# Causal mask for layer 2's row maxima: from TensorE mask products into VectorE's maximum instruction

## What is computed

```python
att = jnp.einsum('bhqd,bhkd->bhqk', q, k) / jnp.sqrt(jnp.float32(D))
mask = jnp.tril(jnp.ones((t, t), dtype=bool))
att = jnp.where(mask, att, jnp.float32(-jnp.inf))
att = jax.nn.softmax(att, axis=-1)
y = jnp.einsum('bhqk,bhkd->bhqd', att, v)
```

## Time and profile before

| | |
|---|---|
| runs of the kernel before | 652.36, 646.97, 653.94 us; median 652.36 |
| the profiled execution, device time | 647.78 us |
| its span, first to last instruction | 646.1 us |
| PE busy | 549.5 us (85%) |
| DVE busy | 396.2 us (61%) |
| ACT busy | 309.1 us (48%) |
| POOL busy | 212.8 us (33%) |
| mean granted TensorE clock | 0.943 |

### The profile page before, as it was taken

The page is one execution under the profiler, slowest core; times in us unless marked ns, Lnnn a source line. Parts: engine busy times, 40 slices in busy tenths (PEclk is TensorE's granted clock), DMA queues, the critical chain, the costliest instruction groups (busy, mean ns, idle before and its releaser), DMA issues.

```text
span 646.1 us, 10027 instructions
## 1 busy us (share of the span) xinstructions
PE 549.5 (85%) x3586; PEld 308.5 (48%) x3586; DVE 396.2 (61%) x932; ACT 309.1 (48%) x589; POOL 212.8 (33%) x276
## 2 busy tenths in 40 slices
PE   2877989787879897799878998999999999899873
PEld 1833435434435454444435555545575446643632
DVE  6368887576767555565765576756656765434463
ACT  2223756575455752466435555554435432564221
POOL 4544543242633731650352311414331110220101
PEclk9576999999899898899989999999999999999998
DMA  8461214211343462201561122125404120000000
GB/s 225 107 171 42 77 38 97 68 53 58 136 113 62 98 156 90 100 35 59 107 166 65 57 51 47 41 80 128 89 14 91 27 51 1 19 2 0 1 17 16
DMA packets 28545, 46.15 MB, mean 71 GB/s; under 512 B 5104, under 2 KB 14352, under 8 KB 27920
## 3 DMA queue, kind: packets, MB, share of 16 engines
q1 hardware_dynamic: 28496, 45.52, 27.4%
HBM read 27.22 MB, written 17.83 MB: 70 GB/s over the span
## 4 chain that ended last, share of the span: by engine, by line
PE 57%; DVE 20%; ACT 6%; issue 5%; SPq 5%; DMA 3%; POOL 3%; POOLq 0%; DVEq 0%; ACTq 0%
PE ps L565 11%; PE ps L522 9%; PE ps L628 8%; DVE NM L1124 6%; PE ps L493 5%; PE ps L490 4%; PE ps L495 4%; PE ps L516 2%; DVE terms L1224 2%; PE ps L650 2%; PE ps L748 2%; DVE stats L1108 2%; PE ps L674 2%; PE ps L572 1%; PE ps L611 1%
## 5 line engine op out<-in xcount | busy, mean ns | idle before, releaser
L1124 DVE TENSOR_REDUCE NM<-ps 128x1 f32<-128x512 f32 (+3 forms) x352 | 219.5, 639 | 120.0 <-PE ps L495 113.0
L785 ACT ACTIVATE PG<-ps 128x512 f32<-128x512 f32 x320 | 181.4, 596 | 160.9 <-PE ps L522 93.6
L522 PE MATMUL ps<-QS,K 128*128 128x512 f32 x320 | 118.6, 455 | 0.6 <-DMA QS<-MP 0.6
L495 PE MATMUL ps<-maskb,identb 128*128 128x128 bf16 x512 | 111.1, 235 | 0.0
L565 PE MATMUL ps<-PG,V 128*32 128x512 f32 (+3 forms) x1024 | 98.4, 458 | 6.7 <-POOL PG L1070 5.2
L493 PE MATMUL ps<-K,QS 96*128 96x256 f32 (+3 forms) x256 | 84.8, 375 | 15.4 <-DVE NM L1124 15.1
L490 PE MATMUL ps<-KS,QS 96*128 96x256 bf16 (+3 forms) x256 | 74.7, 327 | 20.5 <-DVE NM L1124 19.3
L495 PEld LDWEIGHTS ps<-maskb,identb 128*128 128x128 bf16 x512 | 52.4, 102 | 38.7 <-issue 31.4
L522 PEld LDWEIGHTS ps<-QS,K 128*128 128x128 f32 x320 | 51.6, 195 | 39.6 <-issue 21.1
L516 PE MATMUL ps<-QS,KS 128*128 128x128 bf16 (+3 forms) x256 | 63.8, 311 | 6.3 <-DMA QS<-scr 4.2
L1029 POOL TENSOR_TENSOR whole<-terms 128x512 f32<-128x512 f32 x28 | 35.4, 1273 | 101.4 <-DVE terms L1224 65.1
(11 more groups left out here) (153 smaller groups left out, 658.6 us busy)
## 6 DMA issues: line engine op xcount, KB each, us to landing
scr<-QC SPq DMA_DIRECT2D x24, 512.0 KB, 3.1
QS<-scr SPq DMA_DIRECT2D x64, 128.0 KB
QS<-scr_q SPq DMA_DIRECT2D x16, 288.0 KB
KS<-scr_k SPq DMA_DIRECT2D x16, 288.0 KB
QS<-scr SPq DMA_DIRECT2D x64, 64.0 KB
scr_k<-room SPq DMA_DIRECT2D x40, 64.0 KB, 2.1
scr_q<-room SPq DMA_DIRECT2D x24, 64.0 KB, 2.1
x<-in_x SPq DMA_DIRECT2D x4, 256.0 KB, 5.8
```

The source lines that it names most:

```text
L495: return pe.matmul(dst[:, P * (k - 1):P * k], identb[:], maskb[:, 0, :], start=False, stop=True)
L522: mm = pe.matmul(bank.rearrange("p (h q) -> p h q", h=HG), keys[:, SEQ[n] % 2, P * j:P * j + P], QS2[:, heads, P * i:P * i + P], start=(ke ...
L785: act.activation(PG[:, n % 2, unit_place(LAYER[n], (u + k) % UNITS), :], ps[:, ST0 + (u + k) % 3, :], ACT.Exp, scale=scale).then_inc(exp_d ...
L1124: dve.tensor_reduce(dst, src, AX.X, ALU.max, negate=True).then_inc(fill_read, 1)
```

## The change

Layer 1 stays as it is. In layer 2:

- Fills with one head (`i` = 0 and 1, 8 of 11): the mask product is gone. DVE's `tensor_reduce` is replaced by one `tensor_tensor_reduce`: it adds `below` (bf16, in SBUF: zeros for the first key blocks, the mask tile for the last) to the scores, multiplies by -1, writes the result back over the bank, and puts the minimum (so the negated maximum) into `NM`.
- Fills with two and four heads (`i` = 2 and 3, 3 of 11): one mask product for the bank in place of one a head, over the last key block of every head (256 or 512 columns; the mask tile is read again for each head). Only the first product of the bank carries the start flag.
- DVE's maxima of these fills stay `tensor_reduce`.
- `maskb` (128 x 256) becomes `below` (128 x 512), filled by a memset and one cast.

```diff
-        maskb = sb("maskb", [P, 2, P], BF16)
+        below = sb("below", [P, T], BF16)
...
-            def products(dst, n, h, i, k):
+            def products(dst, n, h, i, k, first, alone):
 
                 if LAYER[n] == 1:
                     pe.matmul(dst, QS1[0:MROW, h, P * i:P * i + P], KS1[0:MROW, h, 0:P * k], start=True, stop=False)
-                else:
-
-                    pe.matmul(dst, QS2[0:MROW, h, P * i:P * i + P], K1[0:MROW, SEQ[n] % 2, 0:P * k], start=True,
-                              stop=False)
-                return pe.matmul(dst[:, P * (k - 1):P * k], identb[:], maskb[:, 0, :], start=False, stop=True)
+                    return pe.matmul(dst[:, P * (k - 1):P * k], identb[:], below[:, 3 * P:T], start=False, stop=True)
+                return pe.matmul(dst, QS2[0:MROW, h, P * i:P * i + P], K1[0:MROW, SEQ[n] % 2, 0:P * k], start=first,
+                                 stop=alone, skip_group_check=not alone)
...
-                heads = (1, 1, 2, 4)[i]
+                heads, w = (1, 1, 2, 4)[i], P * (4 - i)
                 for j in range(heads):
-                    w = P * (4 - i)
-                    mm = products(bank[:, w * j:w * j + w], n, h - heads + 1 + j, 3 - i, 4 - i)
+                    mm = products(bank[:, w * j:w * j + w], n, h - heads + 1 + j, 3 - i, 4 - i, j == 0, heads == 1)
+                if LAYER[n] == 2 and heads > 1:
+                    last = bank.rearrange("p (a k) -> p a k", a=heads)[:, :, w - P:w]
+                    mm = pe.matmul(last, identb[:], below[:, 3 * P:T].unsqueeze(1).to_broadcast([P, heads, P]), start=False,
+                                   stop=True, skip_group_check=True)
                 mm.then_inc(score_fill, 1)
...
+                if LAYER[n] == 2 and i < 2:
+                    w = P * (4 - i)
+                    dve.wait_ge(score_fill, n * FILLS + k + 1)
+                    dve.tensor_tensor_reduce(out=bank[:, 0:w], in0=bank[:, 0:w], in1=below[:, T - w:T], scale=-1.0,
+                                             scalar=-NEG, op0=ALU.add, op1=ALU.min, accum_out=NM[:, 3 - i, h:h + 1])\
+                       .then_inc(fill_read, 1)
+                    return
...
-                dve.tensor_copy(maskb[:], masks_sb)
+                dve.memset(below[:, 0:3 * P], 0.0)
+                dve.tensor_copy(below[:, 3 * P:T], masks_sb[:, 0, :])
```

## The result

The changed kernel takes 648.19 us (median of 20 runs, 643.45 to 653.27), the kernel before 652.11 us (median of 20, 646.97 to 657.63). The ratio is 0.9937 with a 95% interval of 0.9911 to 0.9963: 4.1 us less, between 2.4 and 5.8. The forecast was 644 us out of a saving of 8 us; the direction and the range (631 to 660) held, the saving is half of what was forecast, and by the prediction's own bound of 1% it can't be told from no change.

The account below looks back on a forecast made before the run. PE was taken to set the pace in layer 2's fills, with DVE interrupting now and then. 13 us saved on the path, less 1 for DVE and 4 for stalls, gave 8 us off the 652.4 median: 644 us, range 631 to 660.

Parts of the forecast that it names:

- the prediction's own bound of 1%: Whole-kernel time: a measurement can tell a difference from no change only above about 1%, 6.5 us.
- A mask product costs 0.13 us, not its record: PE, layer 2's one-head fills: 0.04 us to the next start plus 0.09 us on the following pair; record 0.23 us.
- The narrow fills: PE, layer 2's fills of two and four heads: one mask product a bank saves 0.14 and about 0.1 us a group.
- Seven tenths of the mask products are on the path: Layer 2 on PE: some 7 in 10 mask products set the time, so 13 of 19 us saved arrive.
- Given back on the dense steps, 4 us: Layer 2 steps without other work: DVE has 0.1 us to spare instead of 0.5, PE's stalls grow by 4 us.
- DVE pays 0.08 us an instruction, 1 us on the path: 128 new DVE instructions in layer 2's one-head fills: 10 us more work, of which 1 us lands on the path.
- The third rival, two passes: One-head fills: the new DVE instruction takes two passes, +0.55 and +0.41 us, making the kernel slower, 670 us; chance 0.16.
- The second rival, the saving is given back: Dense steps: new instruction costs 0.15 to 0.2 us more, or a mask nearer 0.04; 0 to 5 us saved, 650; chance 0.24.
- The signs named: Profile after: 304 mask records, L522 pair 0.45 us, new instruction 0.69 to 0.85, DVE share up 3 points, waits 27.0 to 35.

Follow-up runs that it names:

- W: Kernel before with layer 2's one-head fills stripped of their mask product, plain reduce kept, other fills as before: 651.36 us, ratio 0.9974.
- D: Kernel before with tensor_tensor_reduce in place of the reduce in layer 2's one-head fills, all mask products kept: 653.11 us, ratio 1.0009.

## Why the maximum is late at that fill

The chain of waits of the changed kernel, 514 to 522 us, in order of time:

```profile
516.54 0.59 ACT OT L792
517.14 0.46 ACT CT L943
517.60 0.02 issue
517.62 0.69 DVE CT L1346
...
518.49 0.70 DVE ps L1135
519.19 0.02 issue
519.21 0.10 DVE NM L1135
519.31 0.04 issue
519.35 0.50 PE ps L492 x2
```

DVE's list has a stage's instruction in front of the head's maxima: `combT` (L1346) needs what ACT copies (L943), and ACT does that behind its own copy (L792). DVE idles for it and can't take the maximum that stands behind. PE meanwhile makes two fills and then needs the first one's bank back. The chain begins as these two steps of PE begin (516.54, their first pair at 516.39) and waits for neither of their products, so its length doesn't depend on them. The same chain before, its first and last piece (what stands between has the same order):

```profile
514.88 0.59 ACT OT L791
...
517.53 0.39 PE ps L493
```

That is 2.65 us before and 2.81 after (516.54 to 519.35); some 0.12 of the difference is the readout, 0.70 and 0.10 us of DVE with 0.02 between where it was 0.70. The wait grew by 0.45 us, which is PE's 0.27 us saved and the chain's 0.16.

This is one of the 13 fills with such a wait, and what stands in front of the maxima on DVE is not always the same. The longest wait, 3.73 us at 268.69 before, stands behind additions (L1224) that are held for POOL and then 1.5 us of a norm's statistics (L1108 to L1116), in which DVE is busy. In every one of the 12 before, both maxima stand behind a stage's own instructions. Whatever PE's two steps lose or gain is made up at the third, in these heads and as long as there is a wait; 11 of the 13 are the last head of a group. The forecast saw the ingredients (held foreign instructions, stalls that grow) and not that they meet at one form of fill.

## The prediction, step by step

- **A mask product costs 0.13 us, not its record.** Nearly held: 0.54 became 0.48 for the pair, in other places 0.46 (521.99 to 522.45), and 0.04 went with the product itself; 0.10 to 0.12 us. The reason given for it, a weight load that a short product can't hide, was not tested. In front of the value products 0.07 us went (384 columns: 0.18 + 0.16 = 0.34 us before, about 0.27 after), for which 0.10 was taken. All eight of a group together: 0.76 us (32 x 0.095 in four groups) for the 0.95 of the sum.
- **The narrow fills.** (PE of the kernel before, in order of time, stands below.) The sum gave 0.24 us a group, 3.8 us in all, of which seven tenths are 2.7. By the starts it is less here: the fills of two and four heads took 1.30 us, from the first's start to that of L572,

```profile
517.53 0.39 PE L493 MATMUL ps<-K,QS 96*128 96x256 f32 x1 [0.45 <-DVE NM L1124]
...
518.83 0.61 PE L572 MATMUL ps<-ident_sb,OT 128*128 128x128 f32 x4
```

and now, from 519.35 to 520.62, 1.27. This one place doesn't stand for all: over the stretch of four groups PE's busy time falls by 0.6 to 0.7 us, 0.17 a group, and the stretch becomes shorter by just as much. The runs give 3.4 us (plus or minus 1.3) in all. So nothing of it is lost, and where there is a wait these products stand right behind it, on the path. The right total came from a local price that was too high and a share that was too low, which is luck.
- **Seven tenths of the mask products are on the path.** This is the step that failed for the wide fills. 128 products at 0.095 us are 12 us; the runs say 2.8 us of time, plus or minus 1.3, a quarter. At full clock three fifths arrive in the one stretch and a third in the other, which is also under seven tenths. The chain through the old trace did run over these products, but in some of the odd heads it had a wait just behind them. The wait is the time by which DVE's side was longer than PE's; a shorter PE side only makes it longer. A place on the chain doesn't say what is won when it shrinks, nor, here, what is lost when it grows: 7 us added cost 1.4 (at most 3.3), and 17.6 cost 9.3.
- **Given back on the dense steps, 4 us.** The mechanism is right, PE's idle time, but the term was mis-sized: with the wide mask products gone the idle time is some 8 us higher in the mean of four pages. In the change's own trace 4 us more stand at the fill of two heads, 3.5 by W and 0.7 by D. It was judged from DVE's pace in two dense steps (1.23 us for 1.33), which isn't what held it: the maxima stood behind foreign instructions, some of them held for ACT, POOL or PE. The prediction named these and gave them no number of their own. The 27.0 us that it took as the stalls so far were 10.0 us of the matmul's idle time.
- **DVE pays 0.08 us an instruction, 1 us on the path.** The readout begins 0.61 us into the pass and doesn't delay the next instruction, so the pace stays that of the reduce; the bank is free 0.06 us later. In time: 1.1 us, plus or minus 1.3, as forecast; at full clock 0.4 to 0.6 us in four of the 16 groups, which for 16 like them would be an estimate of 2 us. Here the trace agrees with the Trainium skill (VectorE: DVE Perf Modes, Two Vector instructions with no wait between them) that an operation with an accumulator output is two instructions.
- **The third rival, two passes,** is out: 0.69 us for 512 columns, reading and writing the same bank of PSUM. The rule of the Trainium skill (Vector Engine (DVE) Microarchitecture Reference, Points that are easy to get wrong) on half the rate with two SBUF sources was not put to the test, since one source is PSUM.
- **The second rival, the saving is given back,** had 0 to 5 us, and the measured 4.1 lies in it, as it lies at the lower edge of the forecast's 4 to 12. Neither of its causes came true: the new instruction's pace is the reduce's, and a mask product costs 0.10 us, nearer 0.13 than 0.04. That the number fits both is no sign for its mechanism.
- **The signs named** all came as forecast (304 mask products, 0.69 us, DVE's share in the two stretches 63% for 60%, 32.4 us of waits for 27.0, in the bounds of 27 to 35, both in the double count), and still the saving was half. They were signs that the parts work, not that the saving arrives.

What stays open: of PE's 8 us more of idle time 3.5 stand at the fill of two heads; the rest is spread over other waits, and no run told these apart. In the two stretches at full clock W brings 3.3 us for 76 of its 128 products, more than the 2.8 us (plus or minus 1.3) that the runs give for all of them. Layer 2's first batch, at a granted clock of 0.91 to 0.97, varies too much from page to page to say what W brings there. The one run without masks and with the plain reduce in the wide fills (0.9883) is better than the sum of its parts, 0.9928; its interval reaches to 0.9917. In the stretch of four groups its parts do add up (2.58 us for 1.89 + 0.72), so nothing there supports a gain of the two together.

## What to carry to other kernels

When work is taken from the leading engine in front of a wait of its own, ask what the other side of that wait is made of: if it is a chain on other engines that doesn't start from the work you shorten, the saving is only moved into the wait. Work added there is made up too, up to the wait's length. Before pricing a saving by its share of the chain, list by form where the engine waits, and in how many of the places; a wait concentrated in one form two steps behind the edit is the sign. And a cheap way to test it is to add work there and elsewhere: the same 17.6 us cost 9.3 us in one place and 14.4 in the other. When whole runs are too rough, look for a stretch at the same granted clock in every page and compare its length. Here the third bank for the fills was worth about as much as the change (5.1 us for 4.1), and the two together brought 10.4 us.

## What the runs showed of the hardware

- A DVE instruction with a running result showed as a pass (0.69 us for 512 columns, 0.57 for 384) and a readout of 0.14 us, which overlapped the following instruction's start.
- A mask product of 512 columns that reads the same 128 columns four times took 0.23 us to the next start (520.39 to 520.62), no more than a plain product of 512 columns (516.94 to 517.17).
- A bf16 product of 128 columns behind another one with the same weights cost 0.055 us. Between fp32 products it cost 0.10 to 0.12 us in front of a pair of L522 and 0.07 in front of the value products.
